# Two chained cross attentions: another order of the start, of the first scores and of the last output product, and another layer norm

## What is computed

```python
def _lora_linear(x, W, A, B): return x @ W + 2.0 * (x @ A @ B)
# layer 0
q, k, v = _lora_linear(x, Wq..), _lora_linear(ctx, Wk..), _lora_linear(ctx, Wv..)
attn = softmax(einsum('bhqd,bhtd->bhqt', q, repeat(k)) / 4)
x = x + _lora_linear(attn @ v, Wo, Ao, Bo)
# layer 1
Q, K, V = x @ Wq.T + bq, ctx @ Wk.T + bk, ctx @ Wv.T + bv
attn = softmax(where(mask != 0, Q @ K.T / 4, -inf))
x = x + (attn @ V) @ Wo.T + bo
mu, var = mean(x), mean((x - mu) ** 2)
out = (x - mu) / sqrt(var + 1e-05) * ln_g + ln_b
```

## Time and profile before

| | us |
|---|---|
| median of 3 runs | 1840.78 (1839.41 to 1841.99) |
| the profiled execution | 1840.43 |
| its span in the profile | 1838.6 |

### The profile page before, as it was taken

How to read it: one execution, slowest core, us unless ns; L and a number is a source line. 1 busy time by engine, 2 the same in 40 slices (tenths; PEclk the granted TensorE clock), 3 DMA queues, 4 the chain that set the end, 5 groups by cost and what they waited for, 6 DMA issues and landing times.

```text
span 1838.6 us, 43746 instructions
## 1 busy us (share of the span) xinstructions
PE 1720.4 (94%) x18340; PEld 1171.1 (64%) x18340; DVE 1266.7 (69%) x2743; ACT 1032.9 (56%) x1880; POOL 186.5 (10%) x268
## 2 busy tenths in 40 slices
PE   6699999999999999988999999999999999999985
PEld 3557556675665766655666677767777677767742
DVE  1677777776778787866765677767776777768731
ACT  0055656665666566655654565656665566656651
POOL 1010112002120011021110100001000100001001
PEclk8789999999999999998999999999999999999985
DMA  7822335303362222243523545343544246424400
GB/s 191 250 55 36 64 82 147 64 20 82 82 165 41 34 64 62 37 136 76 104 48 58 104 59 113 43 56 52 106 69 57 41 57 128 57 36 61 57 1 12
DMA packets 65029, 138.12 MB, mean 75 GB/s; under 512 B 12540, under 2 KB 49436, under 8 KB 64832
## 3 DMA queue, kind: packets, MB, share of 16 engines
q1 hardware_dynamic: 64832, 135.33, 36.2%
HBM read 97.84 MB, written 34.89 MB: 72 GB/s over the span
## 4 chain that ended last, share of the span: by engine, by line
PE 86%; DMA 3%; DVE 3%; SPq 2%; ACT 2%; issue 2%; POOL 1%; POOLq 0%; ACTq 0%
PE value L916 22%; PE ring L873 13%; PE work L824 12%; PE work L804 11%; PE score L898 9%; PE score L893 8%; PE work L849 3%; PE work L947 3%; DMA q_stack<-few_rows 2%; PE ring L861 2%; SPq L1351 2%; PE work L832 2%; ACT p_sb L982 1%; PE ring L926 1%; DVE chunk_max L1082 1%
## 5 line engine op out<-in xcount | busy, mean ns | idle before, releaser
L982 ACT ACTIVATE p_sb<-score 124x512 f32<-124x512 f32 (+1 forms) x1664 | 941.8, 597 | 680.4 <-PE score L893 323.8
L1082 DVE TENSOR_REDUCE chunk_max<-ring 128x1 f32<-128x402 f32 x2048 | 1065.7, 569 | 322.4 <-PE ring L873 305.1
L873 PE MATMUL ring<-k_stack,q_stack 64*128 64x402 f32 x2048 | 774.9, 450 | 20.5 <-DVE chunk_max L1082 9.7
L916 PE MATMUL value<-p_sb,v_sb 124*32 124x256 f32 x6656 | 445.4, 391 | 17.4 <-ACT p_sb L982 17.0
L893 PE MATMUL score<-q_stack,k_stack 64*124 64x512 f32 (+1 forms) x832 | 382.5, 514 | 27.7 <-DMA q_stack<-few_rows 26.1
L873 PEld LDWEIGHTS ring<-k_stack,q_stack 64*128 64x128 f32 x2048 | 350.8, 188 | 77.4 <-DVE chunk_max L1082 33.1
L898 PE MATMUL score<-q_stack,k_stack 64*124 64x256 f32 (+1 forms) x1664 | 371.9, 330 | 11.2 <-DMA q_stack<-few_rows 10.4
L824 PE MATMUL work<-wv,ctx_sb 64*124 64x128 f32 x3840 | 377.8, 280 | 2.0 <-ACT v_sb L1004 1.0
L824 PEld LDWEIGHTS work<-wv,ctx_sb 64*124 64x124 f32 x3840 | 347.4, 188 | 9.3 <-PE work L824 3.7
L804 PE MATMUL work<-ctx_sb,wk 64*128 64x402 f32 x1280 | 302.8, 511 | 7.8 <-DMA ctx_sb<-ctxT 7.0
L916 PEld LDWEIGHTS value<-p_sb,v_sb 124*32 124x32 f32 x6656 | 180.2, 110 | 185.1 <-issue 65.4
(11 more groups left out here) (67 smaller groups left out, 574.5 us busy)
## 6 DMA issues: line engine op xcount, KB each, us to landing
k_stack<-k_dram SPq DMA_DIRECT2D x288, 200.1 KB
k_dram<-k_parts SPq DMA_DIRECT2D x60, 402.0 KB, 2.6
ctx_sb<-ctxT SPq DMA_DIRECT2D x24, 992.0 KB, 7.5
k_dram<-k_parts SPq DMA_DIRECT2D x20, 395.0 KB, 2.6
q_stack<-few_rows SPq DMA_DIRECT2D x256, 2.0 KB
wq<-l_Wq SPq DMA_DIRECT2D x2, 1024.0 KB, 10.0
xt_sb<-xT SPq DMA_DIRECT2D x4, 512.0 KB, 11.1
wo<-l_Wo SPq DMA_DIRECT2D x2, 1024.0 KB, 9.4
```

The source lines that it names most:

```text
L873: engine.matmul(ring[bank_of["max", u, half, m]][:, 0:MW], q_stack[rows, u % 3, j, q * P:(q + 1) * P], k_stack[rows, 2 * (z % 3) + (u % 2 ...
L916: done = engine.matmul(value_bank[32 * j:32 * j + 32, 0:S], v_sb[0:tn, seq % 2, i, head * VW:head * VW + 32], p_sb[0:tn, (2 * n + j % 2) % ...
L982: engine.activation(p_sb[0:tn, n % PLACES, :], score_bank[n % 2][0:tn, :], ACT.Exp, scale=SCALE).then_inc(s_exp, 1)
L1082: engine.tensor_reduce(chunk_max[:, u % 2, half, m // NM, m % NM:m % NM + 1], ring[bank_of["max", u, half, m]][:, 0:MW], AX.X, ALU.max)\
```

## The change

Four things are changed.

1. **Start.** SyncE issues the whole context of batch 0 ahead of the weights of the queries. Both key products stand together, then comes the step that loads the stack; the fold and product of the queries, the folds of Wv and Wo follow. The load of Wo is now issued behind that of the stack. The hand-written loop that ran the maxima of unit 0 and the value product of batch 0 is gone; `main` places them, with a budget of 16000 ns to begin with.
2. **Entering a unit.** `enter_unit` no longer forces the remaining maxima and the turn. A score is only offered if the unit's `turn m` is out, and that turn is taken as soon as the modelled time allows. So unit 0 scores with 6 maxima of unit 1 done instead of 12.
3. **Output product.** `att` is turned in two parts: the first three tiles of 128 columns, and the last. For the last batch of layer 1 the first part is turned once six of its eight units are done, and six of the eight pieces of its Wo product run among the scores of the last two units. Its piece order is now three tiles into one pairing of banks and row halves, four into the other, and the last tile into the first; so there are two changes of pairing, each with a wait, instead of one. For the other batches both parts are turned together.
4. **Layer norm.** The bias `bo` is added to x by GpSimd when x is transposed for layer 1, not by VectorE at the end. VectorE now normalises in two scalar_tensor_tensor steps a row block, (x - mean) * g while ScalarE takes the root, and then * rstd + b. GpSimd did the last two steps before.

```diff
     def prologue(self):
         self.fold("k")
         self.step("load lora", "v")
         self.product("k", 0, 0)
+        self.product("k", 0, 1)
+        self.flush()
+        self.step("stack", 0)
         self.fold("q")
         self.step("load w", "wo")
         self.step("load lora", "o")
         self.product("q", 0)
-        self.product("k", 0, 1)
-        self.flush()
-        self.step("stack", 0)
...
-        while sum(self.max_at) < self.CHUNKS + self.LEAD:
-            self.maximum(1)
-            self.maximum(0)
-            for _ in range(4):
-                if ahead and self.piece(*ahead.pop(0)):
-                    break
-            self.ready_turns(self.vector_free)
-        assert not ahead
-        self.flush()
         self.fold("o")
         self.main_products()
...
+        todo += [(3, 0, ("v", 0, g)) for g in v]
+
+        self.budget = 16000.0
...
+        todo.append((UNITS * NT, (UNITS - 3) * NT, ("o", 2 * B - 1)))
...
     def enter_unit(self, u):
...
-        for half in (1, 0):
-            while self.max_at[half] < self.CHUNKS // 2 * (u + 1):
-                self.maximum(half)
-        self.need("turn m", u)
...
-            score = s < total and s - self.values_done < places
+            u = s // NT
+            turned = s >= total or ("turn m", u) in self.emitted
+            entry = None if turned else next((x for x in self.turns if x[1:] == ("turn m", u)), None)
+            if entry and entry[0] <= max(self.free) + 200:
+                self.turn(entry)
+                continue
+            score = s < total and s - self.values_done < places and turned
...
-                    for n, rows, _, k in halves(p):
+                    if p == KT - 1:
+                        e.wait_ge(s_swap, plan.swaps["o", z] - 2)
+                    if p == 2 * KT - 2:
+                        e.wait_ge(s_taken["turn att"], taken["turn att", z, QT - 1, 1])
+                    if p == 2 * KT - 1:
+                        e.wait_ge(s_swap, plan.swaps["o", z])
...
                 elif kind == "sums":
-                    engine.tensor_tensor(y, y, row_bias[:, 1, :], ALU.add).then_inc(s_dve, 1)
...
+                elif kind == "centre":
+                    engine.scalar_tensor_tensor(out=y, in0=y, scalar=moments[:, q, 0:1], in1=row_bias[:, 2, :],
+                                                op0=ALU.subtract, op1=ALU.mult).then_inc(s_centre, 1)
...
+                    engine.scalar_tensor_tensor(out=y, in0=y, scalar=rstd[:, q:q + 1], in1=row_bias[:, 3, :],
+                                                op0=ALU.mult, op1=ALU.add).then_inc(s_out_row, 1)
...
-            load_ctx(0, 0)
+            for c in range(NC):
+                load_ctx(0, c)
             load_lora("q")
             engine.dma_start(wq[:, :, :], by_tile(w0["Wq"])).then_inc(s_w["wq"], 16)
             load_xt(0)
-            for c in range(1, NC):
-                load_ctx(0, c)
```

115 lines of the change are left out of this document (64 added, 51 removed).

## The result

The changed kernel takes 1825.29 us, the median of 4 runs (1822.17 to 1828.56), against 1841.38 (1839.41 to 1846.35) beside it: ratio 0.9909, 95% interval 0.9882 to 0.9935. The profiled execution is the slowest of its four: 1828.56 us, span 1826.7. The span before was 1838.6.

A forecast was written before the change was run, and what follows sets the result against it. TensorE, busy 94% of the span, was taken to set the pace in the middle, with waits and serial work at the ends. The terms -6.6 + 1.5 - 4.5 + 3.5 + 9.3 + 2.5 - 14.3 + 4.7 = -3.9 gave 1836.5 us, range 1826 to 1843.

The forecast's parts named there:

- start and entering: Start and unit entries, with unit 8's wait and clock: -6.6 + 1.5 - 4.5 + 3.5 + 9.3 + 2.5 us.
- Wo product: Last two units and end: 9.5 us saved at the end, 4.7 us lost earlier for the early pieces.
- layer norm: Behind the last value: 1.2 us saved on VectorE's biases, 3.6 us between the variance and the last step.
- Start: Up to the first score: first maximum at 61.4 against 60.72, first score at 89.3 against 95.86, 6.6 us gained.
- Entries: Waits entering units: 9.9 us at seven units against 14.4 before, 4.5 us gained; units 35 and 62 lose 3.5 us.
- Unit 8: Entry of unit 8: maxima rows now behind three context loads and two key writes; 9.3 us wait, 2.5 us lower clock.
- rival 1: Entry of unit 8: rows pass the contexts or find a shorter queue, 10.8 us off, total 1825.7 us; chance 0.14.
- End: Behind the last unit's division: shorter bias, turn, Wo product and layer norm save 14.3 us, bounds 12.5 and 15.5.
- The early pieces of Wo: Last two units: six transposes and six Wo pieces placed earlier cost 4.7 us, bounds 3 and 7.
- Rival 3: Last unit: Wo pieces keep TensorE busier and the clock full, 9 us less, total 1827.5 us; chance 0.07.
- rival 2: Start: unit 0's maxima rows land late; slower by over 3.7 us if first score is past 96.9; chance 0.11.
- Rival 4: Last units: early Wo pieces don't fit the waits, cost 7 not 4.7 us; total 1838.8 or 1843.3 us; chance 0.08.

The follow-up runs named there:

- e1: The kernel before with only the new start and the new entry of units: 1844.72 us, ratio 1.0028.
- e3: The kernel before with only the layer norm change (bias bo by GpSimd early, normalisation by VectorE in two steps): 1832.13 us, ratio 0.9957.
- e8: The changed kernel with the loads of Wo and its low-rank factors issued ahead of the stack's loads: 1824.09 us, ratio 0.9913.
- e4: The changed kernel with context chunks 1 to 3 issued behind, not ahead of, the maxima rows at units 8 and 28: 1814.33 us, ratio 0.9866.
- e2: The kernel before with only the output product change (att turned in two parts, six of eight pieces of the last Wo product early): 1828.93 us, ratio 0.9949.
- e7: The changed kernel with all eight last Wo pieces behind the last value, and six useless pieces of the same size in unit 62: 1835.5 us, ratio 0.9976.
- e6: The changed kernel with all eight pieces of the last Wo product done behind the last value: 1839.69 us, ratio 1.0008.
- e9: The changed kernel with ten useless pieces from unit 62 on and the six early Wo pieces behind them, up to score 8 of unit 63: 1821.68 us, ratio 0.9892.

## Why the prediction was wrong

The sum on record, regrouped by the parts that e1 to e3 ran alone, in us against before:

| part | forecast | measured, medians | measured, in the profiles |
|---|---|---|---|
| start and entering (-6.6 + 1.5 - 4.5 + 3.5 + 9.3 + 2.5) | +5.7 | +3.9 | -0.6 (the fastest of its ten runs) |
| Wo product (9.5 of the end saved, 4.7 for the early pieces) | -4.8 | -11.8 | -11.7 |
| layer norm (1.2 + 3.6) | -4.8 | -8.6 | -5.7 |
| sum | -3.9 | -16.5 | |

**Start: the mechanism right, the gain too small.** The first maximum was forecast at 61.4 and came at 61.34; Wo's factors at 54.0 to 54.2, the fold began at 54.25. The first score was taken at 89.3, with 87.3 as the lower bound, and came at 86.25, below it. The queue's three times, 14.3, 11.2 and 6.7 us, ended at 86.4, which e8 confirms; the 3 us put on top for the rows themselves were too much, as they lay within that time. Of unit 1's 11.2 us a further part was not in the terms at all. Before, the clock was at 0.50 from 83 to 104 us and from 151 to 155; after, behind 70 us, from 84 to 95 only. Three windows of the kernel before:

```profile
90.00:100.00 10.00, 9.67 (x24) 3.46 (x24) 5.28 (x9) 1.68 (x3) 0.00 (x0) 0.50 0.97 140
100.00:110.00 10.00, 10.00 (x71) 6.46 (x72) 6.76 (x13) 5.05 (x9) 0.00 (x0) 0.82 0.01 2
...
150.00:160.00 10.00, 9.94 (x105) 7.30 (x105) 6.39 (x12) 4.07 (x7) 0.00 (x0) 0.83 0.89 120
```

From 60 us to the end of unit 2, before and after, with about the same work in it:

```profile
60.00:182.40 122.40, 115.05 (x1099) 79.10 (x1101) 87.53 (x181) 51.65 (x96) 7.16 (x10) 0.88 0.41 110
```

```profile
60.00:170.95 110.95, 107.11 (x1078) 75.40 (x1077) 81.61 (x173) 50.35 (x94) 7.17 (x10) 0.92 0.39 99
```

Of the 11.5 us, 3.5 are idle time of TensorE and 7.9 busy time. Most of that is the clock, which was at 0.50 for 12.3 us less, worth up to 6.2. With the waits of the earlier trace rows gone, 3.75 us, the forecast for unit 2 is -8.9; measured is -11.5. The sum had no term for the clock behind the first score.

**Entries: right.** Forecast for units 4, 5, 6, 7, 9, 17 and 26 were waits of 1.4, 1.2, 0.6, 2.6, 2.1, 0.5 and 1.5 us; measured 1.49, 1.24, 0.64, 2.90, 2.11, 0.44 and 0.99. Units 35 and 62: 1.5 and 2.0, measured 1.56 and 1.42. Counting the work between turn and score in the list, against 4.3 us, is a good method.

**Unit 8: right.** Wait 9.60 for 9.3. The DMA engines are full from 300 to 316 us. Between the ends of units 6 and 7 the change lost 14.3 us where 11.8 were put for the wait and the clock; but only 8.2 us of them go with the order of the queue, by e4, where rival 1 had priced it at 10.8. Rival 1 and the overtaking of small DMAs behind it have fallen. The Trainium skill (DMA: Bandwidth & Descriptors, Queues, rings and completion order) says that completion is not FIFO for the issuing engine. At unit 8 no overtaking shows: the rows of 8 KB, issued at 301.62, landed at about 312, when the 3 MB of contexts and keys ahead of them were in (the last at 310.4) and the stack behind them had begun to load.

**End: nearly right.** 13.7 us saved against 14.3. The last eight matmuls took 4.25 us instead of 3.4, at half clock; from the variance to the last step on VectorE it is 3.0 us, 2.9 forecast. No GpSimd step is left there.

**The early pieces of Wo: this step failed.** The prediction put them at +4.7 us and reasoned that they cost their own time, or the excess over TensorE's waits. In e2 units 62 and 63 became 4.8 us shorter with them, 9.5 us off the term; by the medians of e2 the whole part is 7.0 us off, more than half of the 12 us that the forecast lacked. In the two profiles of the changed kernel the two units take 53.3 and 49.1 us, against 52.6 before, so the 4.7 us show in neither. Rival 3 named the mechanism, with a price of 9 us, and was given 0.07; its 1827.5 us lie near the result, in part by luck, since the layer norm and the start gave more than it assumed. The argument against it was that nothing is put into the last eleven tiles. That argument was the error: in e2 the last early piece stands at 1785 us, and the full clock lasts over the tiles behind it until 1804. Each tile at full clock takes 1.8 us instead of 2.5. The prediction had both of these numbers in one group of rows and took the place where the clock falls for fixed, when it was a result of the order.

**Layer norm: a term too small.** 6.0 us in the profile of e3 behind the last value, 4.8 forecast. Why the medians give 8.6 stays open: ten runs of e3 spread over 8 us, and no profile here shows which stretch makes the 2.6 us.

Slower by rival 2 was refuted: the first score was at 86.25 and not past 96.9. Rival 4 was refuted by e2.

## What to carry to other kernels

Before counting a step's time, look at the granted clock of the stretch in which it stands: where an engine waits in short pauses and the clock is low, added work can be free, and work moved there can gain more than its own time. In a queue that many transfers share, put the small one that somebody waits for ahead of the large ones that nobody needs yet, but check each large one that you push back for its own first user. And a wait of a queue's engine is also an order: take it away, and what stood behind it comes first.

## What the runs showed of the hardware

- The same instructions took between 1822.17 and 1828.56 us. Two profiles were equal to 0.05 us for 250 us, and parted where the clock stayed low for a different time behind the same wait.
- Useless matmuls made a kernel faster: e7 against e6 4.2 us by the medians, though no row of the two profiles shows where. In e9 forty of them cost nothing, and unit 63 took 22.2 us.
- Four DMAs of 2 KB in a queue of their own landed after 5.7 to 7.4 us with 3 MB of another queue under way, against 1.6 us in the median.
